# Causal masks of a self-attention moved from TensorE to VectorE, and the last multiply moved to GpSimd

## What is computed

```python
q = (x @ Wq.T + bq).reshape(B, T, H, D)
k = (x @ Wk.T + bk).reshape(B, T, H, D)
v = (x @ Wv.T + bv).reshape(B, T, H, D)
scores = jnp.einsum('bqhd,bkhd->bhqk', q, k) * attn_scale[0]
mask = _chunk_mask(T, CHUNK)
scores = jnp.where(mask[None, None], -jnp.inf, scores)
attn = jax.nn.softmax(scores, axis=-1)
out = jnp.einsum('bhqk,bkhd->bqhd', attn, v).reshape(B, T, C)
```

## Time and profile before

| | us |
|---|---|
| median of 3 runs | 3613.83 |
| lowest and highest | 3609.27, 3616.67 |
| the profiled execution | 3648.24 |
| its span, first to last instruction | 3646.3 |

### The profile page before, as it was taken

The page is one execution under the profiler, slowest core; times in us unless marked ns, Lnnn a source line. Parts: engine busy times, 40 slices in busy tenths (PEclk is TensorE's granted clock), DMA queues, the critical chain, the costliest instruction groups (busy, mean ns, idle before and its releaser), DMA issues. The chain is left out here.

```text
span 3646.3 us, 63793 instructions
## 1 busy us (share of the span) xinstructions
PE 3162.4 (87%) x19105; PEld 2060.6 (57%) x19105; DVE 2269.5 (62%) x4409; ACT 1380.1 (38%) x3155; POOL 1512.0 (41%) x1081
## 2 busy tenths in 40 slices
PE   8998989899898998999796999996888882999990
PEld 4444454454444444454344777774777672888880
DVE  3655646565565655556354888884566673777775
ACT  2443434444353443435222666663000000444441
POOL 3342423434242332425322333432466664566661
PEclk8999999999999999999898999997999996999995
DMA  4122120322202122220472121122112112889996
GB/s 119 39 67 71 42 74 24 81 58 67 71 21 79 39 67 72 53 53 9 131 255 87 60 67 62 62 65 96 40 52 58 54 52 84 224 253 250 252 252 209
DMA packets 188688, 344.00 MB, mean 94 GB/s; under 512 B 36153, under 2 KB 53946, under 8 KB 187450
## 3 DMA queue, kind: packets, MB, share of 16 engines
q1 hardware_dynamic: 132282, 242.51, 23.3%
q0 software_dynamic: 28800, 48.43, 5.9%
q10 hardware_dynamic: 27392, 50.34, 3.7%
HBM read 206.96 MB, written 83.89 MB: 80 GB/s over the span
## 5 line engine op out<-in xcount | busy, mean ns | idle before, releaser
L584 DVE TENSOR_REDUCE sa_pmax<-sa_w 128x1 f32<-128x512 f32 (+3 forms) x1280 | 684.7, 603 | 349.0 <-PE sa_w L383 210.4
L526 ACT ACTIVATE sa_probs<-sa_s 128x512 f32<-128x512 f32 (+3 forms) x1280 | 610.8, 537 | 731.1 <-PE sa_s L420 366.0
L329 POOL TENSOR_TENSOR sa_both<-sa_probs 128x2048 f32<-128x2048 f32 (+2 forms) x160 | 589.8, 3687 | 652.5 <-PE sa_pv L444 639.3
L380 PE MATMUL sa_w<-sa_parts 96*128 96x512 f32 (+3 forms) x1280 | 510.5, 450 | 103.7 <-DVE sa_pmax L584 49.4
L417 PE MATMUL sa_s<-sa_parts 128*128 128x512 f32 (+3 forms) x1280 | 471.3, 420 | 19.3 <-ACT sa_probs L526 13.7
L380 PEld LDWEIGHTS sa_w<-sa_parts 96*128 96x128 f32 x1280 | 240.2, 196 | 316.9 <-DVE sa_pmax L584 145.5
L1358 POOL DMA_INDIRECT token_and_weight_of_slot<-rt_entry,rt_sl x256 | 255.2, 997 | 152.4 <-DVE rt_entry L1527 77.1
L417 PEld LDWEIGHTS sa_s<-sa_parts 128*128 128x128 f32 x1280 | 244.0, 197 | 116.3 <-ACT sa_probs L526 68.5
L435 PE MATMUL sa_pv<-sa_probs,sa_values 128*32 128x512 f32 (+3 forms) x2560 | 278.9, 555 | 0.0
L1184 ACT ACTIVATE xa_sm<-xa_sm,xa_nmax 128x154 f32<-128x154 f32 x512 | 208.8, 410 | 64.3 <-DVE xa_nmax L1128 64.3
L1728 POOL DMA_INDIRECT scratch_residual<-ex_y,ex_target x90 | 174.1, 1935 | 124.5 <-DMA scratch_residual<-ex_y,ex_target 94.8
(11 more groups left out here) (243 smaller groups left out, 5907.5 us busy)
## 6 DMA issues: line engine op xcount, KB each, us to landing
ex_w<-in_w SPq DMA_DIRECT2D x138, 512.0 KB
sa_parts<-sa_halves SPq DMA_DIRECT2D x384, 128.0 KB, 2.4
sa_xt<-in_xT SPq DMA_DIRECT2D x32, 1024.0 KB
scratch_attention_T<-sa_oT SPq DMA_DIRECT2D x32, 256.0 KB, 2.2
on_at<-scratch_attention_T SPq DMA_DIRECT2D x32, 256.0 KB, 3.1
on_xr<-in_x SPq DMA_DIRECT2D x32, 256.0 KB, 3.3
scratch_x<-on_xn ACTq DMA_DIRECT2D x32, 256.0 KB, 2.1
scratch_x_T<-on_xnT ACTq DMA_DIRECT2D x32, 256.0 KB, 3.3
```

Source lines behind the costliest of these rows:

```text
L329: pool.tensor_tensor(both[:, :, 0:w], probs[:, even, :, 0:w], probs[:, odd, :, 0:w], ALU.add).then_inc(both_ready, 1)
L380: mm = nc.tensor.matmul(ps[:, 0:w], qparts[0:3 * HD, h, q0:q0 + P], kparts[0:3 * HD, h, k0:k0 + w], start=True, stop=s != 0)
L526: nc.scalar.activation(probs[:, r % NPB, h, 0:w], sbank[n % NSB][:, 0:w], ACT.Exp).then_inc(exp_done, 1)
L584: dve.tensor_reduce(pmax[:, j * GH + h, s:s + 1], wbank[b][:, 0:width_], AX.X, ALU.max).then_inc(work_free[b], 1)
```

## The change

- The two mask matmuls, L383 (512 of them) and L420 (512), and the bf16 identity go.
- For segment s = 0, VectorE's maximum becomes a `tensor_tensor_reduce`: it adds a float32 mask `maskS` of 512 columns to the bank, writes the sum back to the bank, and accumulates the maximum. A semaphore increment stands before it.
- For each diagonal round, VectorE runs a new `cut`: the minimum, in place, of the 4 heads' last 128 columns of `probs` with a tile `maskT` that holds 0 where masked and 3.0e38 elsewhere. There are 16 a group. Those of a pair run in the following pair, behind the maxima of its first round and ahead of those of its second. TensorE's `weighted` and GpSimd's `add_pair` wait for the cut in place of the exponential.
- The maxima of chunks 2 and 3 are spread over one round fewer, so that the last pair of c = 1 and of c = 2 has none.
- `normalize` on VectorE keeps the reciprocal, now into two buffers; the multiply (`multiply`) goes to GpSimd's queue: for chunks 0, 1 and 2 behind `add_pair` of (3, 2), (3, 4) and (3, 6), and for chunk 3 behind `add_pair` of the next group's (0, 0). SyncE's code is unchanged.

```diff
@@ -23,6 +23,7 @@
 QB = CH // P
 NEG = -1.0e30
 LOWEST = -3.0e38
+HUGE = 3.0e38
 
 
 @contextmanager
@@ -88,7 +89,7 @@
         if c == 0:
             return spread_over(1, EARLY, 32, 0, 3, k)
         if c < NC - 1:
-            return spread_over(c + 1, 0, len(segments(c + 1)), 0, rounds(c) - 1, k)
+            return spread_over(c + 1, 0, len(segments(c + 1)), 0, rounds(c) - 2, k)
         return spread_over(0, 0, 16, 7, 11, k) + spread_over(1, 0, EARLY, 12, 16, k)
 
     def others_in(c, k):
@@ -128,6 +129,9 @@
 
     rest_pairs = [p for p in range(NR // 2) if rounds(round_at[2 * p][0]) - round_at[2 * p][1] <= QB]
     NREST = len(rest_pairs)
+
+    diagonal = [r for r, (c, k) in enumerate(round_at) if rounds(c) - k <= QB]
+    NDIAG = len(diagonal)
 
     NSB = 3
     NPB = 4
@@ -161,12 +165,11 @@
         mhi = sb("mhi", [P, QB * GH], F32R)
         mcol = sb("mcol", [P, QB, GH, HD])
         raw = sb("raw", [P, NC, CH]); den = sb("den", [P, NC, CH])
-        rden = sb("rden", [P, CH])
+        rden = sb("rden", [P, 2, CH])
         oT = sb("oT", [P, 2, CH])
-        identb = sb("identb", [P, P], BF16)
         identf = sb("identf", [P, P])
-        maskS = sb("maskS", [P, P], BF16)
-        maskT = sb("maskT", [P, P], BF16)
+        maskS = sb("maskS", [P, CH])
+        maskT = sb("maskT", [P, P])
         wbank = [ctx.enter_context(nc.psum_tensor(f"sa_w{i}", [P, CH], F32)) for i in range(NWB)]
         sbank = [ctx.enter_context(nc.psum_tensor(f"sa_s{i}", [P, CH], F32)) for i in range(NSB)]
         pvbank = [ctx.enter_context(nc.psum_tensor(f"sa_pv{i}", [P, CH], F32)) for i in range(2)]
@@ -182,8 +185,8 @@
         mstep = sem("mstep"); mcol_ready = sem("mcol_ready")
         shift_ready = sem("shift_ready")
         s_ready = sem("s_ready"); exp_done = sem("exp_done"); pv_done = sem("pv_done")
-        both_ready = sem("both_ready"); rest_copied = sem("rest_copied"); ones_done = sem("ones_done")
-        pv_free = sem("pv_free"); den_free = sem("den_free"); raw_used = sem("raw_used"); rden_ready = sem("rden_ready"); o_ready = sem("o_ready")
+        cut_done = sem("cut_done"); both_ready = sem("both_ready"); rest_copied = sem("rest_copied"); ones_done = sem("ones_done")
+        pv_free = sem("pv_free"); den_free = sem("den_free"); raw_used = sem("raw_used"); rden_ready = sem("rden_ready"); rden_free = sem("rden_free"); o_ready = sem("o_ready")
         o_stored = [kept_semaphore(nc, sems, f"o_stored{i}") for i in range(2)]
         block = ctx.enter_context(nc.Block())
 
@@ -289,26 +292,27 @@
                 n += 1
                 ins.then_inc(pool_step, 1)
                 pool.wait_ge(pool_step, n)
-            for t in (identb, identf, maskS, maskT, mcol):
+            for t in (identf, maskS, mcol):
                 step(pool.memset(t[:], 0.0))
+            step(pool.memset(maskT[:], HUGE))
             step(pool.memset(pmax[:], LOWEST))
             step(pool.memset(ones[:], 1.0))
             for t in (qparts, kparts):
                 step(pool.memset(t[3 * HD:P].bitcast(F32), 0.0))
             step(pool.memset(kparts[3 * HD:3 * HD + 2].bitcast(F32), 1.0))
-            for t in (identb, identf):
+            for t in (identf,):
                 step(pool.affine_select(out=t[:], in_=t[:], compare_op=ALU.not_equal, fill=1.0, base=0,
                                         pattern=[[-1, P]], channel_multiplier=1))
             H = P // 2
             step(pool.memset(maskS[H:P, 0:H], NEG))
-            step(pool.memset(maskT[0:H, H:P], NEG))
+            step(pool.memset(maskT[0:H, H:P], 0.0))
             for a in (0, H):
 
                 v = maskS[a:a + H, a:a + H]
                 step(pool.affine_select(out=v, in_=v, compare_op=ALU.is_ge, fill=NEG, base=0,
                                         pattern=[[-1, H]], channel_multiplier=1))
                 v = maskT[a:a + H, a:a + H]
-                step(pool.affine_select(out=v, in_=v, compare_op=ALU.is_ge, fill=NEG, base=0,
+                step(pool.affine_select(out=v, in_=v, compare_op=ALU.is_ge, fill=0.0, base=0,
                                         pattern=[[1, H]], channel_multiplier=-1))
             pool.sem_inc(consts_set, 1)
 
@@ -320,7 +324,10 @@
                 c, k = round_at[2 * p]
                 wide, w = width(c, kbs(c)[k]), width(c, kbs(c)[k + 1])
                 pool.wait_ge(ones_done, it * NPAIR + (p + 1))
-                pool.wait_ge(exp_done, it * NU + (NSB + 2 * GH * (p + 1)))
+                if 2 * p + 1 in diagonal:
+                    pool.wait_ge(cut_done, it * NDIAG + (diagonal.index(2 * p + 1) + 1))
+                else:
+                    pool.wait_ge(exp_done, it * NU + (NSB + 2 * GH * (p + 1)))
                 apart(pool, passed)
                 if wide > w:
                     pool.tensor_copy(both[:, :, w:wide], probs[:, even, :, w:wide]).then_inc(rest_copied, 1)
@@ -328,9 +335,30 @@
                     apart(pool, passed)
                 pool.tensor_tensor(both[:, :, 0:w], probs[:, even, :, 0:w], probs[:, odd, :, 0:w], ALU.add).then_inc(both_ready, 1)
 
-            with pool.Fori(0, ITERS) as it:
-                for p in range(NPAIR):
-                    add_pair(it, p)
+            pool.sem_inc(raw_used, NC)
+            pool.sem_inc(rden_free, 2)
+
+            def multiply(it, c):
+                pool.wait_ge(o_stored[c % 2], it * (NC // 2 * 16) + (c // 2 * 16 + 16))
+                pool.wait_ge(rden_ready, it * NC + (c + 1))
+                pool.wait_ge(pv_free, it * NC + (c + 2))
+                apart(pool, passed)
+                pool.tensor_tensor(oT[:, c % 2], raw[:, c], rden[:, c % 2], ALU.mult).then_inc(o_ready, 1)
+                pool.wait_ge(o_ready, it * NC + (c + 1))
+                pool.sem_inc(raw_used, 1)
+                pool.sem_inc(rden_free, 1)
+
+            def pair(it, p, more, behind):
+                add_pair(it, p)
+                c, k = round_at[2 * p]
+                if c == NC - 1 and 2 <= k < 2 + 2 * (NC - 1):
+                    multiply(it, k // 2 - 1)
+                if p == 0 and behind is not None:
+                    multiply(behind[0], NC - 1)
+
+            pair(0, 0, True, None)
+            each_from_second(pool, pair)
+            multiply(ITERS - 1, NC - 1)
 
         @block.tensor
         def _(pe):
@@ -377,11 +405,8 @@
                 k0 = q0 + s * CH
                 w = min(CH, SEQ - k0)
                 ps = bank(it, ("m", c, n))
-                mm = nc.tensor.matmul(ps[:, 0:w], qparts[0:3 * HD, h, q0:q0 + P], kparts[0:3 * HD, h, k0:k0 + w],
-                                      start=True, stop=s != 0)
-                if s == 0:
-                    mm = nc.tensor.matmul(ps[:, 0:P], identb[:], maskS[:], start=False, stop=True)
-                mm.then_inc(work_ready, 1)
+                nc.tensor.matmul(ps[:, 0:w], qparts[0:3 * HD, h, q0:q0 + P], kparts[0:3 * HD, h, k0:k0 + w],
+                                 start=True, stop=True).then_inc(work_ready, 1)
 
             def shift(it, i, c):
                 ps = bank(it, ("s", c))
@@ -413,12 +438,8 @@
 
                 pe.wait_ge(exp_done, it * NU + (n + 1 if n else NSB))
                 ps = sbank[n % NSB]
-                diag = kb < QB * (chunk_q(c) + 1)
-                mm = nc.tensor.matmul(ps[:, 0:w], kparts[:, h, kb * P:(kb + 1) * P], qparts[:, h, q0:q0 + w],
-                                      start=True, stop=not diag)
-                if diag:
-                    mm = nc.tensor.matmul(ps[:, w - P:w], identb[:], maskT[:], start=False, stop=True)
-                mm.then_inc(s_ready, 1)
+                nc.tensor.matmul(ps[:, 0:w], kparts[:, h, kb * P:(kb + 1) * P], qparts[:, h, q0:q0 + w],
+                                 start=True, stop=True).then_inc(s_ready, 1)
 
             def weighted(it, p):
 
@@ -429,7 +450,10 @@
                     if k == 0:
                         pe.wait_ge(pv_free, it * NC + (c + 1))
                         pe.wait_ge(v_ready, it * NC + (c + 1))
-                    pe.wait_ge(exp_done, it * NU + (NSB + GH * r + GH))
+                    if r in diagonal:
+                        pe.wait_ge(cut_done, it * NDIAG + (diagonal.index(r) + 1))
+                    else:
+                        pe.wait_ge(exp_done, it * NU + (NSB + GH * r + GH))
                     for h in range(GH):
                         a = HD * h
                         mm = nc.tensor.matmul(pvbank[0][a:a + HD, 0:w], values[:, kb, h, :], probs[:, r % NPB, h, 0:w],
@@ -542,7 +566,6 @@
             for b in range(NWB):
                 dve.sem_inc(work_free[b], 1)
             dve.sem_inc(den_free, 1)
-            dve.sem_inc(raw_used, NC)
             dve.wait_ge(scl_loaded, 16)
 
             def scale_queries(i):
@@ -581,8 +604,14 @@
                 width_ = min(CH, SEQ - chunk_q(c) * CH - j * P - s * CH)
                 b = bank_of(it, ("m", c, n))
                 dve.wait_ge(work_ready, ready_at(it, ("m", c, n)))
```

(34 more changed lines are left out.)

## The result

| | before | after |
|---|---|---|
| median of the runs, us | 3615.25 | 3700.74 |
| lowest and highest | 3609.27, 3617.05 | 3697.88, 3704.14 |
| profiled execution, us | 3648.24 | 3702.42 |
| end of the self-attention in that execution (TensorE's first weight load behind it) | 1775.6 | 1862.8 |

The change makes the kernel slower: the ratio is 1.0233, with a 95% interval of 1.022 to 1.0245, or +85.5 us on the medians. The sign and the range of the prediction hold. The forecast was 3743, so +129 was about 43 us too much. Inside the self-attention the profiled executions differ by +87.2 us, which agrees with the timed loss. What follows the self-attention is the same code, yet it took 1832 to 1881 us in the profiled executions of this study (1870.7 in the one before, 1837.9 in the one after), so the two profiled executions differ by only 54 us as wholes.

The account below looks back on a forecast made before the run. VectorE was taken to bound c = 1 and c = 2, TensorE c = 3 and (0,0). Terms +77 (seams), +64 (c = 1 and 2), -10, -1 and -1 gave +129 on 3613.8: 3743 us, range 3655 to 3845.

Parts of the forecast that it names:

- seam: Between groups, (0,2) grows 10.0 us as copies wait for the store, plus 1.0 for slow clock; times 7 seams: +77.
- c = 1 and c = 2, the rest: Pairs bound by VectorE: 3.2 + 1.3 + 7.0 - 2.8, less 0.7 for masks; +8.0 us a group, +64.
- (0,0): Pair held to be bound by TensorE: 12 or 13 masks go, -1.3 us a group, times 8: -10.
- c = 3: Masks gone up to (3,12) give -3.3 us, (3,14) costs +3.1; -0.2 a group, -1 in all.
- the third of the chain: In (0,2), VectorE's maxima end 9.3 us into the pair, from 9.8 before.
- the second low stretch of the clock: TensorE's clock falls again behind the wait at the seam, priced at +1.0 us each, times 7 seams.
- The moved maxima: Seven segments leave (1,6), six leave (2,10), into pairs VectorE bounds, at 0.54 us average: +7.0 us a group.
- The masked maximum: Sum and maximum in one: +0.1 us for 32 exposed a group, +3.2; dear rival +0.6 us, 3871 us, 8%.
- Pair (3,14): Keeps its maxima, then cuts, copy, add and L444: 9.9 us against 6.83, +3.1 a group.
- The store was waited for: Rival at the seam: chunk 3's store is not waited for, the 77 us fall away, +52 stay: 3666 us, 10%.
- the rival's price of 99 us: Rival: cuts wait out GpSimd adds, 3.1 us in 4 places a group, times 8: +99, 3842 us, 5%.
- The faster rival: TensorE is the bound after all and VectorE's additions fit in idle time in c = 1 and 2: about 3590 us, 6%.

## Why the prediction was right, and where its sizes were off

The direction and the two causes held; four terms of the sum were mis-sized. The column on the right is the difference of the table's columns before and after.

| term | forecast | trace |
|---|---|---|
| seam: (0,2), and (1,0) beyond what the narrow spread does to it | +77 | +40.6 + 10.7 = +51 |
| c = 1 and c = 2, the rest | +64 | +25 |
| (0,0) | -10 | -4 |
| c = 3 | -1 | +16 |
| sum | +129 (with -1 elsewhere) | +89 (with +1 behind the last pair) |

*The seam.* The mechanism was right, step by step. The run with the multiply first confirms the place, -62 us, and the run with the multiply alone, -21 us from the same place, that it takes the cuts as well. No run moved the copies ahead of the store in SyncE's order, which would test that link by itself. The step that failed is the third of the chain: "VectorE's maxima end ... 9.8 in; without the multiply (0.73) and with the dearer maxima, 9.3". I carried over the 3.54 us of the branch from the earlier trace rows and took off the multiply alone. The branch hides under the reciprocal once nothing waits behind it, so the first copy was issued 14.0 us into the pair (532.19 less 518.18) and not 17.7. The 12 copies then took 7.7 us and not 8.7, and TensorE was released at 23.56, not 28.5. The same hidden branch by itself is worth -16 us in the kernel before, by the run with the later branch.

*What follows the seam.* I priced the second low stretch of the clock at +1.0 a group, +7. In (1,0) the clock is 0.77 in the window shown, and the pair takes 20.49 us against 18.43 with the narrow spread alone and a clock of 1.00. The trace gives +10.7 for all groups; the term was somewhat too small.

*c = 1 and c = 2.* "about 6.7 against 8.15 and 8.05, so -2.8" was the failed step. The emptied pairs are 5.84 and 5.66, because the cuts start before the pair does: of the two of (1,6), one is over and the other has 0.38 us left in the window. They gave 44.7 us and not 22; about 7 of the 44.7 are four such pairs of the kernel before that ran at a clock of 0.82 or 0.83. The moved maxima were nearly right in sum, +56 forecast and +47 measured with (1,0) counted, but not in place: (1,4) is longer by 0.1 us and (2,2) by 0.6, where "longer by 1 to 2 us" was forecast, while (1,0) and (1,2) are longer by 1.6 to 2.0 at a clock of 1.00. So (1,4), with VectorE busy for 7.36 of 10.04 us, had room for two more maxima. The masked maximum was too dear by half: +26 forecast, at most +12.5 by the run with plain maxima, since the read overlaps. The cuts in (2,0) were right, +10.4 forecast and 78.2 - 66.8 = +11.4 measured.

*c = 3 and (0,0).* "In c = 3 and in (0,0) it is TensorE" was half the truth, and the third failed step. I read TensorE's busy 7.87 of 7.87 us as the sole bound and didn't look for VectorE's pace in the same pair, though its eight maxima in 5.12 us were in the trace. The masks' gain in c = 3 was forecast at -26; without masks at all it is -10.3 ((3,8) to (3,14)), and with masked maxima in their place -4.2 in (3,8) to (3,12). In (0,0) it was forecast at -10; it is -4 with the change and -5 without masks at all, in seven groups. Pair (3,14) came out as forecast: 9.59 against 9.9, and its chain is in the trace of the kernel after:

```profile
723.32 1.29 DVE L660 TENSOR_TENSOR sa_probs<-sa_probs,sa_maskT 128x512 f32<-128x512 f32 x2
...
724.77 0.61 POOL L333 COPY sa_both<-sa_probs 128x512 f32<-128x512 f32 x1 [6.96 <-DVE sa_probs L660]
725.56 3.44 POOL L336 TENSOR_TENSOR sa_both<-sa_probs 128x1536 f32<-128x1536 f32 x1 [0.18 <-POOL sa_both L333]
```

*The rivals.* The store was waited for. The masked maximum was not dear. The cuts seldom meet an add: 118 of the 128 took 0.68 us, and ten took 2.7 to 3.5. Eight of the ten are the first cut for (2,10), one in each group, here in the kernel after with the add that it meets:

```profile
647.82 4.06 DVE L660 TENSOR_TENSOR sa_probs<-sa_probs,sa_maskT 128x512 f32<-128x512 f32 x2 [1.51 <-ACT sa_probs L550]
...
647.26 3.47 POOL L336 TENSOR_TENSOR sa_both<-sa_probs 128x1536 f32<-128x1536 f32 x1 [0.18 <-POOL sa_both L333]
```

The first of the two cuts took 3.46 us and ended 0.5 us behind the add. The rule of the Trainium skill (SBUF — State Buffer, "SBUF: two separate sides"), that a VectorE operation with two SBUF inputs and a GpSimd one that reads SBUF exclude each other for the whole instruction, agrees with this. It cost nothing, since the next add still waited for TensorE when these cuts were done. So cuts of 2 us or more, which the prediction named as a sign of being wrong, are there, but off the path, and the rival's price of 99 us was not paid. The faster rival, that TensorE is the bound after all, failed: taking the masks away, and nothing else, makes the kernel slower, and with 16 of them kept to hold the clock in (2,10), no more than 8 us faster.

## What to carry to other kernels

An instruction that a store waits for should stand in its engine's queue ahead of work that waits for something late. Here the multiply behind an add saved 21 us while the add waited for nothing late, and cost 62 us more than ahead of it once the add waited for the cuts. So when a wait is added to one instruction, look at what stands behind it in the same queue. Before a saving on a busy engine is counted, look in the same window for a second engine that already runs at its own pace. And where a loop closes, put the branch where the engine still has a long instruction running and waits for nothing behind it.

## What the runs showed of the hardware

- Removing 1024 small matmuls made the kernel 0.57% slower, since the granted clock of TensorE fell to 0.70 in (2,10) and 0.83 in (1,6), two pairs in which it idles for part of the time. Keeping 16 a group restored 1.00 in (2,10) in all eight groups, and 32 in (1,6) in seven of eight.
- VectorE's loop branch costs 3.1 to 3.5 us when the engine has nothing running, and nothing visible under a 3.35 us reciprocal.
- A minimum over 128x512 of SBUF on VectorE took 0.68 us alone and 3.46 beside a GpSimd add of 3.47 us.
- A sum and maximum over a PSUM bank of 512 with the sum written back takes 695 ns, against 684 for a maximum that writes nothing, and its accumulator read of 141 ns overlaps the next instruction.
